# A graph neural network chain on one core: signals once a round, one row load and one-hot step a round, dense loads in another order

## What is computed

```python
# L0: self term and sum of neighbours
x = layernorm(x + relu(x @ W + segment_sum((x @ M)[src], dst)))
# L1: two GAT layers, 4 heads, softmax over the incoming edges
z = x @ W;  e = leaky_relu(el[src] + er[dst]);  alpha = softmax_by_dst(e)
x = elu(segment_sum(z[src] * alpha, dst) + x + b)          # twice, then layernorm of the residual
# L2: three HGT layers, 8 heads of 32, typed W_Q, W_K, W_V, edge-typed W_E, mu
scores = sum(Q[dst] * kt, -1) / sqrt(32) * mu[edge_type]
agg = segment_sum(V[src] * softmax_by_dst(scores), dst)
x = layernorm(x + agg @ Wo + bo);  h = gelu(x @ w1 + b1) @ w2 + b2;  x = layernorm(x + h)
# L3: relational layer, 8 relations, block-diagonal weights
x = layernorm(x + sum_r blockmm(segment_sum_r(x[src] * edge_weight), W_r))
```

## Time and profile before

| what | value |
|---|---|
| runs | 7738.59, 7749.21, 7752.94 us |
| the profiled execution | 7760.78 us, span 7758.8 us |
| granted clock of TensorE, mean of the span | 0.732 of full speed |
| busy, share of the span | PE 59%, DVE 47%, ACT 43%, POOL 49% |

### The profile page before, as it was taken

The page is one execution under the profiler, slowest core; times in us unless marked ns, Lnnn a source line. Parts: engine busy times, 40 slices in busy tenths (PEclk is TensorE's granted clock), DMA queues, the critical chain, the costliest instruction groups (busy, mean ns, idle before and its releaser), DMA issues. The chain is left out here.

```text
span 7758.8 us, 85682 instructions
## 1 busy us (share of the span) xinstructions
PE 4547.2 (59%) x23719; PEld 3578.0 (46%) x23719; DVE 3657.2 (47%) x8546; ACT 3309.8 (43%) x7523; POOL 3818.8 (49%) x4057
## 2 busy tenths in 40 slices
PE   4445444434446344565666795666796666796444
PEld 3444333323334233354444694555595554574333
DVE  7222211134445244475777545777544777662112
ACT  2333232234445244454444464444364444355555
POOL 1655566645552555524555334555334555314665
PEclk6555666666667676677777797778797778797777
DMA  1111233433333333425555324555414555423334
GB/s 58 46 45 51 64 90 91 88 97 98 97 98 65 100 98 98 95 81 178 175 170 176 82 70 149 171 171 172 95 66 147 169 170 178 116 82 112 92 90 91
DMA packets 395895, 850.11 MB, mean 110 GB/s; under 512 B 93952, under 2 KB 204445, under 8 KB 392045
## 3 DMA queue, kind: packets, MB, share of 16 engines
q0 software_dynamic: 213760, 613.91, 29.4%
q1 hardware_dynamic: 177306, 227.54, 9.2%
q10 hardware_dynamic: 4435, 3.84, 0.2%
HBM read 738.97 MB, written 106.04 MB: 109 GB/s over the span
## 5 line engine op out<-in xcount | busy, mean ns | idle before, releaser
L630 POOL DMA_INDIRECT ring<-tab_kv,idx_i x1392 | 1320.6, 949 | 1123.0 <-PE pp L693 476.0
L630 POOL DMA_INDIRECT ring<-tab_z,src_i x928 | 887.8, 957 | 697.8 <-PE pp L693 285.6
L854 DVE TENSOR_TENSOR acc<-acc,pp 128x264 f32 x1160 | 493.5, 425 | 1203.4 <-DMA mus<-in_L_gnn_mu 446.8
L693 PE MATMUL pp<-ring,X 128*128 128x264 f32 x2784 | 910.5, 477 | 190.7 <-issue 124.4
L997 PE MATMUL pp<-ring,oh 128*128 128x256 f32 x1856 | 591.6, 485 | 724.3 <-issue 326.8
L658 PE MATMUL pq<-Qs,oht 128*128 x6960 | 723.6, 249 | 270.8 <-issue 160.8
L997 PEld LDWEIGHTS pp<-ring,oh 128*128 128x128 f32 x1856 | 445.3, 248 | 870.8 <-issue 507.7
L658 PEld LDWEIGHTS pq<-Qs,oht 128*128 128x128 bf16 x6960 | 576.7, 106 | 482.8 <-issue 322.9
L693 PEld LDWEIGHTS pp<-ring,X 128*128 128x128 f32 x2784 | 609.9, 233 | 342.9 <-issue 174.3
L846 DVE TENSOR_TENSOR ring<-ring,pc 128x1024 f32<-128x1024 f32 x580 | 704.1, 1215 | 131.1 <-remote 49.4
L1089 DVE TENSOR_TENSOR acc<-acc,pp 128x256 f32 x464 | 195.2, 421 | 1120.7 <-DMA tab_z<-zs 342.8
(11 more groups left out here) (313 smaller groups left out, 8806.0 us busy)
## 6 DMA issues: line engine op xcount, KB each, us to landing
oht<-lo_row SPq DMA_DIRECT2D x290, 256.0 KB
tab_kv<-X SPq DMA_DIRECT2D x100, 384.0 KB
drow<-in_dst SPq DMA_DIRECT2D x25, 1024.0 KB
tab_h<-hs SPq DMA_DIRECT2D x25, 1024.0 KB, 4.1
ring<-tab_kv,idx_i POOLq DMA_INDIRECT x1392
tab_kv<-room SPq DMA_DIRECT2D x50, 384.0 KB
ring<-tab_z,src_i POOLq DMA_INDIRECT x928
ring<-tab_y,src_i POOLq DMA_INDIRECT x464
```

Source lines behind the costliest of these rows:

```text
L630: nc.gpsimd.indirect_dma_start(out=ring[:, w % RW, c, :], out_offset=None, in_=table, in_offset=bass.IndirectOffsetOnAxis(ap=idx[:, w * WC ...
L693: last = nc.tensor.matmul(pp[p % 2][:, 0:W8], oh[:, w % 2, 2 * p + c, :], ring[:, w % RW, 2 * p + c, 0:W8], start=(c == 0), stop=(c == 1))
L854: nc.vector.tensor_tensor(a, a, pp[p % 2][:, 0:W8], ALU.add).then_inc(s_acc, 1)
```

## The change

- Sort: `ys` has four tiles and goes to HBM two tiles a DMA, 13 DMAs in place of 26. The 16 one-hot steps of a round increment once, after the last.
- `attend`, loads and one-hots: one row load of 2048 a round (`columns_of(w)`: slots 0 and 1, or 0 and 2 in turn) in place of two of 1024; `columns` and `rows` once a round, with one Relu over 2048 numbers each and 16 Abs in a row. In DOTS `rows` comes ahead of `columns`, in SUMS behind. SP waits until half the `qrows` of the round before are done.
- `attend`, signals: `s_red` once a round in DOTS; the chain on DVE increments 8 times in place of 12, the rescaling once in place of twice.
- `attend`, order of PE in SUMS: N0 behind G2, N2 ahead of G6.
- `sum_edges`: PE increments once for two pairs, and POOL, ACT and DVE wait by twos.
- `dense_stage` with `front`: SP loads bo (with a semaphore of its own) and Wo first, then ln1_g, ln1_b, b2, w1, b1, w2, ln2_g, ln2_b; out_g and out_b only in dense 3. The loads of WK and WE go to ACT's queue. Their use on PE, ACT and DVE comes one step u later. The waits follow: POOL's first add for bo alone, and for b2 at its first use, DVE for three rows at u = 1 and for the rest at u = 5.

```diff
                     for u in range(2, NSORT):
                         load(u)
-                        if u >= 3:
-                            y_out(u - 3)
-                    for t in range(NSORT - 3, NSORT):
+                        if u >= 4 and u % 2 == 0:
+                            y_out(u - 4)
+                    for t in range(NSORT - 4, NSORT, 2):
                         y_out(t)
...
+                            counted = nc.vector.scalar_tensor_tensor(eq[:, k, :], drow[:, u % 2, k, :], dcol[:, k:k + 1], tri[:, :],
+                                                                     ALU.is_equal, ALU.mult, accum_out=same[:, k:k + 1])
+                        L.do(counted)
...
-    ORDER_T_SUMS = order("l G0 G1 N0 G2 G3 N1 G4 C1 G5 G6 N2 G7 N3 C2 C3 C4")
+    ORDER_T_SUMS = order("l G0 G1 G2 N0 G3 N1 G4 C1 G5 N2 G6 G7 N3 C2 C3 C4")
...
+            def columns_of(w):
+                return oht[:, 0:2 + w % 2:1 + w % 2, :]
...
-                    for k in range(2 * NW):
-                        if k >= LOB:
-                            e.wait_ge(s_q, 2 * (k - LOB + 1))
-                        e.dma_start(oht[:, k % LOB, :], lo_row[:, k * NHALF:(k + 1) * NHALF].to_broadcast([P, NHALF])
-                                    ).then_inc(s_lo[k % LOB], 16)
+                    for w in range(NW):
+                        if w:
+                            e.wait_ge(s_q, w * NQ - 2)
+                        e.dma_start(columns_of(w), lo_row[:, 2 * w * NHALF:2 * (w + 1) * NHALF].rearrange("o (h n) -> o h n", h=2)
+                                    .to_broadcast([P, 2, NHALF])).then_inc(s_lo, 16)
...
+                    def columns(w):
+                        e.wait_ge(s_lo, 16 * (w + 1))
+                        cols = columns_of(w)
+                        nc.scalar.activation(cols, cols, ACT.Abs, scale=-1.0, bias=part_c[:, :]).then_inc(s_ac, 1)
+                        e.wait_ge(s_ac, w + 1)
+                        nc.scalar.activation(cols, cols, ACT.Relu, scale=-1.0, bias=1.0).then_inc(s_ev, 1)
...
+                    def rows(w):
+                        e.wait_ge(s_pp, (w + 1) * NPR)
+                        for c in range(WC):
                             last = nc.scalar.activation(oh[:, w % 2, c, :], iota_row[:, :], ACT.Abs, scale=-1.0,
                                                         bias=lo_s[:, w * WC + c:w * WC + c + 1])
...
+                        e.wait_ge(s_ab, w + 1)
+                        nc.scalar.activation(oh[:, w % 2, :, :], oh[:, w % 2, :, :], ACT.Relu, scale=-1.0, bias=1.0).then_inc(s_oh, 1)
...
                     for w in range(NW):
+                        if dots:
+                            rows(w)
                         if w + 1 < NW:
-                            columns(2 * w + 2)
-                        rows(w, 0)
-                        rows(w, 1)
-                        if w + 1 < NW:
-                            columns(2 * w + 3)
+                            columns(w + 1)
+                        if not dots:
+                            rows(w)
...
-                    c_base, c_per, m_per = C.n, 12, 2
+                    c_base, c_per, m_per = C.n, 8, 1
...
-                        e.wait_ge(s_red, w * NQ + q + 1)
...
+                        if q == NQ - 1:
+                            last.then_inc(s_red, 1)
...
-                        C.do(nc.vector.transpose(two(colF[:, :]), at_c(outF, 1)))
+                        nc.vector.transpose(two(colR[:, :]), at_c(outR, 3))
+                        nc.vector.tensor_copy(inF[:, :, 0], outF[:, :, 2 * WC])
+                        nc.vector.tensor_tensor(dg[:, :], outF[:, :, 1], outR[:, :, 2], ALU.subtract)
                         C.wait(6)
...
-                            e.wait_ge(s_p, p + 1)
+                        if p >= RB * BP and p % 2 == 0:
+                            e.wait_ge(s_p, p // 2 + 1)
                             e.sem_inc(s_go, 1)
...
+                            if k % 2:
+                                last.then_inc(s_p, 1)
...
-                            e.wait_ge(s_p, u * BP + (k + 1 + RB * BP))
+                            if k % 2 == 0:
+                                e.wait_ge(s_p, u * (BP // 2) + (k // 2 + 1 + RB * BP // 2))
...
-                    if not end:
-                        for t in range(NT):
-                            e.dma_start(WK[t * HW:(t + 1) * HW, :, :],
-                                        io["L2_gnn_W_K"][nxt, t, :, :, :].rearrange("h d x -> d h x")).then_inc(s_wp, 16)
...
+                    row = lambda name: io["L2_gnn_" + name][l:l + 1, :]
                     if front:
-                        row = lambda name: io["L2_gnn_" + name][l:l + 1, :]
+                        e.dma_start(bo, row("bo").to_broadcast([P, D])).then_inc(s_bo, 16)
                         e.dma_start(Wo[:, :, :], io["L2_gnn_Wo"][l, :, :].rearrange("(h p) m -> p h m", p=P)).then_inc(s_wo, 16)
-                        for k, name in enumerate(("bo", "b2", "ln1_g", "ln1_b", "ln2_g", "ln2_b")):
+                        for k, name in ((2, "ln1_g"), (3, "ln1_b"), (1, "b2")):
                             e.dma_start(rows[:, k, :], row(name).to_broadcast([P, D])).then_inc(s_gb, 16)
-                        for k, name in ((6, "out_g"), (7, "out_b")):
-                            e.dma_start(rows[:, k, :], io["L2_gnn_" + name].unsqueeze(0).to_broadcast([P, D])).then_inc(s_gb, 16)
                         e.dma_start(w1[:, :, :], io["L2_gnn_w1"][l, :, :].rearrange("(h p) m -> p h m", p=P)).then_inc(s_w1, 16)
...
                         e.dma_start(w2[:, :, :], io["L2_gnn_w2"][l, :, :].rearrange("(f p) m -> p f m", p=P)).then_inc(s_w2, 16)
+                        for k, name in ((4, "ln2_g"), (5, "ln2_b")):
+                            e.dma_start(rows[:, k, :], row(name).to_broadcast([P, D])).then_inc(s_g2, 16)
+                        for k, name in ((6, "out_g"), (7, "out_b")):
+                            if end:
+                                e.dma_start(rows[:, k, :], io["L2_gnn_" + name].unsqueeze(0).to_broadcast([P, D])).then_inc(s_g2, 16)
...
-                                e.wait_ge(s_gb, 128)
+                                e.wait_ge(s_bo, 16)
...
+                            if t == 0:
+                                e.wait_ge(s_gb, 48)
...
-                        if not end and u == 2:
+                        if not end and u == 3:
...
-                        if not end and u == 3:
+                        if not end and u == 4:
...
+                    if front and not end:
+                        for t in range(NT):
+                            e.dma_start(WK[t * HW:(t + 1) * HW, :, :],
+                                        io["L2_gnn_W_K"][nxt, t, :, :, :].rearrange("h d x -> d h x")).then_inc(s_wp, 16)
...
-                                e.wait_ge(s_gb, 128)
+                                e.wait_ge(s_gb, 48)
+                            if u == 5:
+                                e.wait_ge(s_g2, 16 * NG)
```

102 lines of the change are left out of this document (44 added, 58 removed).

## The result

The changed kernel takes 7794.36 us (median of six runs, 7783.24 to 7817.24), the kernel before 7753.49 (six runs, 7738.59 to 7770.45). The ratio is 1.0056, 95% interval 1.0036 to 1.0076: slower by 41 us. That is small, but the whole interval lies above 1. The forecast was 7724, so faster; the range of 7560 to 7800 holds the measured time only because it reaches far to both sides. The rival on the other side said 7783. Of all executions in this document one is left out of the ratios: it is of `dots_columns_first_again`, took 10365 us at a granted clock of 0.585, and nothing on record explains it.

What follows compares the result with a forecast made beforehand. Rounds were taken as bound by POOL's gather stream plus increments let through some 2 us after it runs dry. Dense loads gave -25, all else 0: 7760.8 to 7736 profiled, median 11.6 lower, so 7724; range 7560 to 7800.

Steps and rivals of the forecast that it cites:

- parts 2, 4 and 5: In attend: row load and one-hots, fewer signals on DVE, PE's order in SUMS; each put into the sum as 0.
- The dense loads: Dense 1, 2 and 3: loads in order of use let DVE's add start sooner; -8.2, -9.4, -7.0, sum -24.6 us.
- The term of +1.9 each for the WK transposes: Dense 1 and 2: transposes once in PE's idle time now delay the pipeline, +1.9 us each; -28.4 in all if they hide.
- Part 5: PE's order in SUMS: N0 behind G2 neutral, N2 ahead of G6 delays G6; taken as 0, the delay priced as a rival.
- slower rival: SUMS: G6 behind N2 is held, A6 and D1 run after the release; 1.1 us in 54 rounds, +59, 7783; chance 0.29.
- parts 2 and 4: DOTS: single row load and 2048-column one-hots, 0 (-0.5 to +1 us a round); fewer DVE signals, 0 down to -10.
- +1 us x 87: DOTS: PE's N0 late behind ACT's column step, +1 us in each of 87 rounds, 7811 in all; chance 0.05.
- Relief: Sum stages and attend: fewer increments free the path; -284 with the loads, 7465, or 7637 with sum stages alone; chance 0.22.
- the trace's 27.3 us: SUMS round before: 16 gathers, 20.0 us, plus the time until the chain behind the late increment gives POOL work.
- the 84.6 us of rows 6: First SUMS stage's start: DVE's first step waits 84.6 us during 64 gathers; taken to point to POOL's DMAs, not increment count.

Runs made afterwards that it cites:

- dots_columns_first_again: Changed kernel with ACT's column step ahead of the row steps in DOTS, run again beside the kernel before on another chip; -0.4%.
- group 1: First of six groups of follow-up runs, each on one chip with the kernel before beside them; here the kernel before took 7772.16 us.
- sums_order_back: Changed kernel with PE's order in SUMS as before (N2 behind G6, N0 behind G1); 7754.56 us against 7772.16 for the kernel before.
- dense_loads_alone: Kernel before with the change's dense_stage and nothing else; 7741.36 us against 7772.16.
- changed_third: Changed kernel run again, on a chip where increments are not late; -0.4% against the kernel before.
- sums_order_alone: Kernel before with PE's new order in SUMS and nothing else, on a chip where increments are not late; ratio 0.9999.
- dots_columns_first: Changed kernel with ACT's column step ahead of the row steps in DOTS; 7696.58 us against 7772.16 for the kernel before in its first run.
- changed_again: Changed kernel run once more, on a chip where the kernel before took 6376.52 us; ratio 0.9962.

## Why the prediction was wrong

The step that failed is the 0 that the sum has for `attend`, in its parts 2, 4 and 5: in the first result's profile these stages take 20 us more in SUMS and 65 in DOTS, three times what the loads give back. For SUMS the runs show what happened in the rounds, for DOTS they do not show the cause.

1. *The dense loads*, -24.6 and rounded to -25 in the sum, were right: -28.0 in the first result, and the whole of the change on prompt chips, -21 to -24. Stage by stage -10.2, -11.1 and -6.7 stand against -8.2, -9.4 and -7.0. The term of +1.9 each for the WK transposes was too careful; without it the sum had its upper end, -28.4.
2. *Part 5 at zero* is the step that failed in the SUMS stages. The slower rival's mechanism is in the trace of the first result: A6 and D1 behind the release, a round of 28.3 us where 28.4 was written down. It belongs to the new order, since D1 is behind the long wait in 23 to 25 of 28 rounds in all three late profiles with that order, and in 0 to 13 in the three with the old one and POOL's waits as before. But its price, 1.1 us in each of 54 rounds, was wrong too. The two stages gave +20 and not +59 in the first result, and on the chip of group 1 the new order's stages were the shorter ones, 771 against 787. What a round takes is not set by D1's place alone: beside rounds of 28.3 us there are some of 24, and some of 19 to 22 next to some of 33 to 37. So the rival came near with 7783 in part by luck: its 59 us were to come from SUMS, and most of the 85 came from DOTS.
3. *DOTS at zero* (parts 2 and 4) failed by more: +65 over three stages, for which the prediction had +1 us x 87 with a chance of 0.05. The size is near, the mechanism is not: N0 was to be late behind ACT's columns, and it is not. A6 and D1 stand behind the release in 25, 23 and 25 rounds, where before 17 to 19 rounds had it so. Which edit in `attend` does this, if one does, is not shown. On the chip of group 1 the three DOTS stages sum to 2398 us with the changed DOTS code (sums_order_back) and 2391 with that of before (dense_loads_alone), and neither has the uniform rounds.
4. *Relief* did not come. The sum stages, with half of PE's increments, are 1.4 and 1.1 us shorter, and POOL still stops there. The chance of 0.22 for it stretched the range downwards by 160 us, to no use. Its sum had a slip besides: 14 stops of 5.7 us are 80 us and not 87, and the waits of the first sum stage are 100 us in 40 stops.
5. What no step of the prediction asked is whether rounds that hang on late increments repeat from chip to chip. It took the trace's 27.3 us for a property of the program, and the 84.6 us of rows 6 for a sign that POOL's own DMAs set the hold. The prompt chips have the same stream of gathers and 19 us there, so the stream alone does not bring it. With the same code on late chips the changed kernel is +0.56% once and -0.67% once. So points 2 and 3 describe where the first result's time went, but its sign is not the program's alone; what makes the rounds fall into the 28.3 us pattern on one chip and not on another stays open.

In the sum stages 232 fewer increments went with 1.4 and 1.1 us less on the late chip of the first result. On one prompt chip these stages take 580.6 and 584.6 us with the change (changed_third) and 580.8 and 584.7 without (sums_order_alone). By the Trainium skill (TensorE: Matmul & The Clock Gate, "The cost: per-tile semaphore tail") the increments would be 6 us, an estimate. The late chips cannot tell so small a term from scatter, and on the prompt chip, where POOL's stream sets the stage, it does not show. Halving PE's increments also left POOL's stops in place, which speaks against the relief. The Trainium skill's warning (VectorE: DVE Perf Modes, section on the TRN2 errata), which the prediction put beside that rival, is of a deadlock by increments at a high rate; no run here stopped.

No version beats all others everywhere. `dots_columns_first` was never slower than the kernel before, 0.9926 on a late chip and 0.9960 to 0.9963 in three prompt draws. With a single late draw that is no proof that it stays so.

## What to carry to other kernels

Where a trace shows an engine waiting for something long finished, a re-ordering by a microsecond can move steps across the release, to either side, so such a term needs both signs and a time on several chips before it is believed. A gain that is read from waits for DMAs at a stage's start (here, one add waiting for eight loads of which it needs one) came out alike on both kinds of chip: 10, 11 and 7 us on a late one, 10, 9 and 7 on a prompt one. Compare kernels on the same chip, and ask first whether the kernel before takes the same time there.

## What the runs showed of the hardware

The kernel before took 7753 to 7772 us (medians) in three draws of a chip and 6373 to 6378 in four others. The difference lies in the stages with POOL's indirect DMAs: rounds of 27 us against 20.5, sort 671 against 548 us, first sum 674 against 581, while the time between DOTS 1 and 2 is about the same in the changed kernel (366 and 367, 368 to 373 us). The mean granted clock of the profiled executions was 0.73 to 0.75 on the first kind and 0.76 to 0.80 on the second.

On the slower chips increments of PE, DVE and ACT are seen late while POOL streams gathers, and come through 2 to 3 us after it has run dry: DVE's adds shown above wait 5.6 to 8.2 us in a round, its first step of a SUMS stage 78 to 87 us. On the others none of the increments of `agg` is over 2 us late, beside the same stream. The gathers themselves are not slower: one keeps POOL busy for 957 ns in SUMS on the first chip and 951 in changed_again on a prompt one, and in the first SUMS stage the mean packet of their queue takes 181 ns in the kernel before and 184 in sums_order_alone. What in the chip, or around it, makes the difference is not shown; nothing in the program tells the two kinds apart.
